# Idle matmuls where TensorE's array work runs low, and a new order of the steps, in a two-layer transformer kernel

## The reference

```python
x = x + 0.5 * ffn0(layernorm(x))            # gated, hidden 512, ternary weights times scales
x = x + attn0(layernorm(x))                 # linear attention, no softmax
x = x + 0.5 * ffn0(layernorm(x))            # the same weights again
x = x + 0.5 * experts(layernorm(x))         # 8 experts of rank 64, two picked by token 0 of a sequence
x = x + attn1(layernorm(x))                 # 16 heads of width 8, RoPE, causal softmax
x = x + 0.5 * experts(layernorm(x))
# ffn0: silu(x W1) * (x W2) -> gelu(. H1) -> gelu(. H2) -> . W3
```

## Time and profile before

| | |
|---|---|
| median of 3 runs | 642.38 us (640.28 to 642.96) |
| the profiled execution: its time | 645.81 us |
| its span, first to last instruction | 644.0 us |
| TensorE busy | 607.3 us (94%) |
| VectorE, ScalarE, GpSimd busy | 476.0, 479.9, 233.1 us |
| mean granted clock of TensorE | 0.984 |

### The profile page before, as it was taken

How to read it: one execution, slowest core, us unless ns; L and a number is a source line. 1 busy time by engine, 2 the same in 40 slices (tenths; PEclk the granted TensorE clock), 3 DMA queues, 4 the chain that set the end, 5 groups by cost and what they waited for, 6 DMA issues and landing times.

```text
span 644.0 us, 17311 instructions
## 1 busy us (share of the span) xinstructions
PE 607.3 (94%) x6902; PEld 472.0 (73%) x6902; DVE 476.0 (74%) x1298; ACT 479.9 (75%) x832; POOL 233.1 (36%) x354
## 2 busy tenths in 40 slices
PE   4899999999999999999999999998898999999997
PEld 3677878888887887888877887665565667766675
DVE  6667566765766778656777668898899787788964
ACT  5799778787788787887878776745778466778792
POOL 1402303312312526403337346756654542331032
PEclk9999999999999999999999999999999896899999
DMA  9300000000000001100003003413444423223002
GB/s 295 110 2 1 0 1 2 1 2 1 1 1 1 1 2 49 50 2 2 0 7 92 1 22 119 135 47 132 147 131 128 143 77 114 88 90 101 23 13 60
DMA packets 41230, 35.24 MB, mean 55 GB/s; under 512 B 2952, under 2 KB 37032, under 8 KB 41148
## 3 DMA queue, kind: packets, MB, share of 16 engines
q1 hardware_dynamic: 41148, 34.12, 16.8%
HBM read 19.17 MB, written 14.68 MB: 53 GB/s over the span
## 4 chain that ended last, share of the span: by engine, by line
PE 63%; DVE 14%; ACT 11%; issue 6%; POOL 2%; DMA 2%; SPq 1%; POOLq 0%; DVEq 0%; ACTq 0%
PE PSA L1009 20%; PE PSA L1013 19%; PE PSA L1248 5%; DVE MX L1438 3%; PE PSA L1028 3%; DVE G L1316 3%; ACT PB L1587 2%; ACT PSA L1492 2%; DVE RA L1431 2%; PE PSA L1236 2%; PE PSA L1227 1%; ACT G L1488 1%; PE PSA L1172 1%; PE PSA L1192 1%; PE PSA L1165 1%
## 5 line engine op out<-in xcount | busy, mean ns | idle before, releaser
L1009 PE MATMUL PSA<-ah,WH 128*128 128x512 f32 x320 | 130.5, 408 | 2.4 <-DVE al L1321 1.5
L1013 PE MATMUL PSA<-al,WH 128*128 128x512 f32 x320 | 125.1, 391 | 0.0
L1492 ACT ACTIVATE PSA<-PSA,SC 128x512 f32<-128x512 f32 x128 | 84.6, 661 | 50.8 <-PE PSA L1013 50.3
L1438 DVE TENSOR_REDUCE MX<-PSA 128x10 f32<-128x640 f32 x128 | 101.2, 815 | 17.7 <-PE PSA L1199 17.3
L1009 PE MATMUL PSA<-bh,WH 128*128 128x512 f32 x256 | 105.7, 413 | 3.1 <-DVE G L1316 3.1
L1013 PE MATMUL PSA<-bl,WH 128*128 128x512 f32 x256 | 100.2, 391 | 0.0
L1587 ACT ACTIVATE PB<-PSA 128x640 f32<-128x640 f32 x128 | 84.8, 703 | 20.3 <-PE PSA L1236 19.1
L1321 DVE TENSOR_TENSOR al<-PSA,ah 128x512 fp32r<-128x512 f32 x64 | 44.0, 688 | 56.5 <-ACT ah L1499 56.4
L1614 POOL TENSOR_SCALAR VE<-MV 128x4 f32<-128x4 f32 x46 | 11.2, 244 | 205.4 <-DVE MV L1291 205.4
L1009 PEld LDWEIGHTS PSA<-ah,WH 128*128 128x128 f32 x320 | 60.2, 188 | 17.6 <-DVE al L1321 3.8
L1013 PEld LDWEIGHTS PSA<-al,WH 128*128 128x128 f32 x320 | 60.2, 188 | 11.8 <-issue 1.0
(11 more groups left out here) (168 smaller groups left out, 1281.6 us busy)
## 6 DMA issues: line engine op xcount, KB each, us to landing
KQ<-dk SPq DMA_DIRECT2D x32, 192.0 KB
KQ<-dq SPq DMA_DIRECT2D x32, 192.0 KB
dk<-CB SPq DMA_DIRECT2D x16, 192.0 KB, 2.5
dq<-CB SPq DMA_DIRECT2D x16, 192.0 KB, 2.6
X<-in_x SPq DMA_DIRECT2D x8, 256.0 KB, 6.8
dk<-CB SPq DMA_DIRECT2D x16, 128.0 KB, 1.9
dq<-CB SPq DMA_DIRECT2D x16, 128.0 KB, 2.7
W<-in_w SPq DMA_DIRECT2D x3, 512.0 KB, 5.7
```

Source lines behind the costliest of these rows:

```text
L1009: e.matmul(o, WH[:, col:col + 128], hi, start=first, stop=False)
L1013: return e.matmul(o, WH[:, col:col + 128], low, start=False, stop=last)
L1438: e.tensor_reduce(MX[:, u % 2, :, :].rearrange("p t (l g) -> p l t g", l=2)[:, :, :, g], PSA[:, b:b + 2, 0:320].rearrange("p l (t k) -> p ...
L1492: e.activation(bank(b), bank(b), ACT.Gelu, scale=SC[:, k:k + 1]).then_inc(a_gelu, 1)
```

## The change

Four things. `fill` gets a larger share of a planned gap (FILLED 0.85, reserve SPARE 0.06 us plus the changes of tile shape) and a second form: between steps of 64-row tiles, when banks 6 and 7 are both unheld, four matmuls of 64x64 tiles and 256 columns take the place of the 128x128 one, so that the shape stays. A new function `hold` is called before each step of TensorE once the first stream of feed-forward work has ended: it adds up, by the new table WORK, what array work the plan has laid in the last HOLD[0] us and, where this is less than the share HOLD[1], it puts idle matmuls in front of the step, up to 0.5 us, and moves the planner's clock by them. The prices of some steps change (`expert`, `qk`, `value`, `vexp`, `max_out`, `pass2`, `weighed`, `upright`, `proj`, `lone_x`, `lone_g`). And SHIFT is a new set, so the order of all steps after the first ones is another. Three waits name their source's number instead of their own, which lets the half chunks of the ending pass each other.

```diff
@@ -69,23 +69,28 @@
     "att0": [("P", 1.08, 1.15), ("V", 0.6, 0.68)],
     "table": [("P", 1.1, 1.3), ("V", 0.6, 0.68)], "logit": [("P", 0.37, 0.55), ("V", 0.85, 0.95)],
     "tanh": [("A", 0.09, 0.2)], "gate": [("V", 0.14, 0.23)], "pick": [("G", 2.75, 2.82)], "pick_b": [("G", 1.25, 1.3)],
-    "expert": [("P", 0.42, 0.6), ("V", 0.33, 0.41)],
-    "qk": [("P", 0.95, 1.02), ("V", 1.9, 2.05)], "turned": [("G", 1.23, 1.27)],
+    "expert": [("P", 0.47, 0.66), ("V", 0.33, 0.41)],
+    "qk": [("P", 0.88, 1.06), ("V", 1.9, 2.05)], "turned": [("G", 1.23, 1.27)],
     "cast0": [("A", 0.52, 0.62), ("S", 0.95, 0.95), ("D", 2.5)], "rest0": [("G", 1.11, 1.16)],
     "cast1": [("A", 0.52, 0.62), ("S", 0.95, 0.95), ("D", 2.5)],
     "rest1": [("G", 1.12, 1.16), ("S", 0.95, 0.95), ("D", 2.3)], "reloc": [("S", 2.95, 2.95), ("D", 5.0)],
-    "value": [("P", 0.9, 1.1), ("A", 0.48, 0.59)], "vexp": [("A", 0.6, 0.7)], "rows": [("S", 0.65, 0.65), ("D", 2.0)], "ones": [("G", 1.15, 1.2)],
+    "value": [("P", 0.99, 1.16), ("A", 0.48, 0.59)], "vexp": [("A", 0.83, 0.9)], "rows": [("S", 0.65, 0.65), ("D", 2.0)], "ones": [("G", 1.15, 1.2)],
     "pass1": [("P", 0.225, 0.395), ("V", 0.735, 0.82)], "peak": [("V", 0.32, 0.4), ("A", 0.13, 0.24), ("G", 0.2, 0.26)],
-    "max_out": [("P", 0.22, 0.29), ("V", 0.33, 0.4), ("S", 1.18, 1.18), ("D", 3.8)],
-    "pass2": [("P", 0.22, 0.39), ("A", 0.58, 0.7)], "weighed": [("P", 1.12, 1.21), ("A", 0.27, 0.38)],
-    "upright": [("P", 0.45, 0.6), ("V", 0.65, 0.73)],
-    "flat": [("P", 0.27, 0.44), ("A", 0.27, 0.38)], "proj": [("P", 0.64, 0.71), ("V", 0.33, 0.41)], "store": [("S", 0.9, 0.9)],
+    "max_out": [("P", 0.12, 0.29), ("V", 0.33, 0.4), ("S", 1.18, 1.18), ("D", 3.8)],
+    "pass2": [("P", 0.22, 0.39), ("A", 0.6, 0.7)], "weighed": [("P", 1.13, 1.29), ("A", 0.27, 0.38)],
+    "upright": [("P", 0.49, 0.66), ("V", 0.65, 0.73)],
+    "flat": [("P", 0.27, 0.44), ("A", 0.27, 0.38)], "proj": [("P", 0.54, 0.71), ("V", 0.33, 0.41)], "store": [("S", 0.9, 0.9)],
     "half_stat": [("V", 0.85, 1.0)], "half_power": [("G", 0.8, 0.8)], "half_norm": [("V", 0.5, 0.6)],
     "half_xt": [("P", 0.3, 0.44), ("A", 0.27, 0.38)], "half_expert": [("P", 0.45, 0.71), ("V", 0.33, 0.42)],
     "half_store": [("S", 0.9, 0.9)],
-    "lone": [("P", 0.25, 0.4), ("A", 0.15, 0.2)], "lone_x": [("P", 0.4, 0.55), ("A", 0.15, 0.2)],
-    "lone_m": [("P", 0.2, 0.35), ("V", 0.1, 0.16)], "lone_g": [("P", 0.5, 0.6), ("V", 1.0, 1.1)],
+    "lone": [("P", 0.25, 0.4), ("A", 0.15, 0.2)], "lone_x": [("P", 0.6, 0.83), ("A", 0.15, 0.2)],
+    "lone_m": [("P", 0.2, 0.35), ("V", 0.1, 0.16)], "lone_g": [("P", 1.1, 1.37), ("V", 1.0, 1.1)],
     "lone_power": [("G", 0.7, 0.7)], "lone_df": [("V", 0.07, 0.15)],
+}
+WORK = {
+    "xtf": 0.43, "xta": 0.43, "xtp": 0.43, "up": 0.85, "hid": 0.85, "down": 0.85, "back": 0.43, "gram": 0.85, "half": 0.43,
+    "fold": 0.43, "att0": 0.85, "table": 0.43, "expert": 0.43, "qk": 0.85, "value": 0.85, "pass1": 0.15, "pass2": 0.16,
+    "weighed": 1.07, "upright": 0.43, "flat": 0.21, "proj": 0.43, "half_xt": 0.21, "half_expert": 0.43,
 }
 HOPS = {"P": 0.06, "V": 0.04, "A": 0.04, "G": 0.08, "S": 0.05}
 
@@ -104,27 +109,34 @@
 FIRST = (3, 1.5)
 LEAD = 20
 LONE = 4.0
-FILLED = 0.65
+HOLD = (3.4, 0.42)
+FILLED = 0.85
+SPARE = 0.06
 
...
-    ("after", 0, 2): -0.16, ("after", 0, 6): -0.02, ("after", 1, 7): 0.49, ("attend", 0): -0.02,
-    ("attend", 2): 0.1, ("attend", 3): 0.2, ("attend", 4): -0.16, ("attend", 5): -0.09, ("attend", 6): -0.19,
...
+    ("after", 0, 2): 0.16, ("after", 0, 3): 0.19, ("after", 0, 4): -0.1, ("after", 0, 6): -0.09,
+    ("after", 1, 0): -0.05, ("after", 1, 1): -0.29, ("after", 1, 4): -0.24, ("after", 1, 6): -0.38,
+    ("after", 1, 7): 0.09, ("attend", 0): -0.37, ("attend", 1): -0.15, ("attend", 2): 0.54, ("attend", 5): 0.08,
...
+    ("weigher", 9): 0.23, ("weigher", 10): 0.19, ("weigher", 12): 0.39, ("weigher", 13): -0.65,
+    ("weigher", 14): -0.14, ("weigher", 15): 0.23,
...
@@ -193,7 +205,8 @@
         self.added, self.picked = set(), {}
         self.into = [0, 0]
         self.lasts = 1
-        self.table = self.pe = ""
+        self.table = self.pe = self.last = ""
+        self.worked = []
         self.idle_from = 0.0
         self.lay()
 
@@ -235,28 +248,63 @@
                 t = max(t, later - 0.45 * (name == "up"))
             s0 = max((ready if name in BESIDE else t) + HOPS[eng], self.clock[eng])
             if eng == "P":
-                self.fill(s0)
-                self.idle_from = s0 + us
+                self.fill(s0, kind)
+                s0 = self.hold(s0, kind)
+                self.worked.append((s0, s0 + us, WORK.get(name, 0.0)))
+                self.idle_from, self.last = s0 + us, kind
             self.note(eng, s0, s0 + us, name)
             self.clock[eng] = s0 + us
             t = st.at[eng] = s0 + way[0]
         st.done = max([t] + [st.at[e] for e in st.at if name in BESIDE])
         return st
 
-    def fill(self, t):
-
-        free = {b: f for b, f in enumerate(self.bank) if f}
+    def keep(self, form, n, a, each, banks):
+        if n <= 0:
+            return
+        self.note("P", a, a + each * n, "keep" + form)
+        self.worked.append((a, a + each * n, n * {"h": 0.107, "f": 0.053, "w": 0.107}[form]))
+        k = self.count.get("keep", 0)
+        self.count["keep"] = k + 1
+        self.steps.insert(-1, Step("keep", k, x=n, b=min(banks), b2=max(banks), kind=form,
+                                   emptied=sum((self.bank[b] for b in banks), [])))
+
+    def fill(self, t, kind):
+
+        free = sorted((self.left(f), b) for b, f in enumerate(self.bank) if f)
         if not free or not self.opened:
             return
 
-        each = 0.06 if self.count.get("masks") else 0.23
-        b = min(free, key=lambda b: self.left(free[b]))
-        n = int((t - max(self.idle_from, self.left(free[b]) + 0.06) - 0.15) * FILLED / each)
-        if n > 1:
-            self.note("P", max(self.idle_from, self.left(free[b]) + 0.06), max(self.idle_from, self.left(free[b]) + 0.06) + each * n, "keep")
-            k = self.count.get("keep", 0)
-            self.count["keep"] = k + 1
-            self.steps.insert(-1, Step("keep", k, x=n, b=b, kind="w" if each > 0.1 else "", emptied=free[b]))
+        h = self.last == "h" and self.bank[6] is not None and self.bank[7] is not None
+        h = h and self.left(self.bank[6] + self.bank[7]) <= max(self.idle_from, free[0][0] + 0.1)
+        if h:
+            free = [(self.left(self.bank[6] + self.bank[7]), 6), (0.0, 7)]
+        form = "h" if h else "f" if self.count.get("masks") else "w"
+        each = {"h": 0.125, "f": 0.06, "w": 0.23}[form]
+        own = form if h else "f"
+        a = max(self.idle_from + 0.094 * (self.last != own), free[0][0] + 0.06)
+        n = int((t - a - 0.094 * (kind != own) - SPARE) * FILLED / each)
+        if n > (not h):
+            self.keep(form, n, a, each, [b for _, b in free[:1 + h]])
+
+    def hold(self, t, kind):
+
+        if len(self.dead) < 1 or kind not in "fh":
+            return t
+        done = 0.0
+        for a, z, work in reversed(self.worked):
+            if a < t - HOLD[0] - 4.0:
+                break
+            done += work * max(0.0, min(z, t) - max(a, t - HOLD[0])) / (z - a)
+        free = [b for _, b in sorted((self.left(f), b) for b, f in enumerate(self.bank) if f and self.left(f) + 0.06 < t)]
+        if kind == "h":
+            free = [b for b in free if b > 5]
+        short = HOLD[0] * HOLD[1] - done
+        if short <= 0.05 or len(free) <= (kind == "h"):
+            return t
+        each, work = (0.125, 0.107) if kind == "h" else (0.06, 0.053)
+        n = min(int(short / work + 0.99), int(0.5 / each))
+        self.keep(kind, n, t, each, free[:2 if kind == "h" else 1])
+        return t + each * n
 
     def note(self, eng, a, z, name):
         pass
@@ -1109,7 +1157,7 @@
                                      start=True, stop=True)
                     t.then_inc(p_logit, 1)
                 elif st.name == "half_xt":
-                    w.wait_ge(v_half_xn, n + 1)
+                    w.wait_ge(v_half_xn, st.src.n + 1)
                     emptied(w, st.emptied)
                     for j in range(2):
                         t = e.transpose(PSA[:, b, 128 * j:128 * j + 128], XN[:, st.i, j, :], IDN[:, :])
@@ -1206,8 +1254,14 @@
                         w.wait_ge(g_c, 5)
                     emptied(w, st.emptied)
                     for _ in range(st.x):
-                        ID = IDN if early else IDB
-                        e.matmul(PSA[:, b, 0:128], ID[:, :], ID[:, :], start=True, stop=True)
+                        if st.kind == "h":
+                            for x in range(2):
+                                for h in range(2):
+                                    e.matmul(PSA[64 * x:64 * x + 64, (st.b, st.b2)[h], 0:256], IM[64 * h:64 * h + 64, 0, 0:64],
```

(31 more changed lines are left out.)

## The result

The changed kernel is slower: 649.68 us median of 8 runs (647.91 to 650.17) against 642.51 us of the kernel before (638.05 to 646.95, 8 runs); ratio 1.0111, 95% interval 1.0082 to 1.014. I had forecast 638.5 us in 633.0 to 644.0.

A forecast was written before the change was run, and what follows sets the result against it. Bound: TensorE in the feed-forward chunks, shared in the attention, TensorE alone for 20.6 us at half clock. 645.8 - 6.1 + 1.0 + 0.5 - 1.0 = 640.2 us; middle with 636.8 taken: 638.5 us, range 633.0 to 644.0.

The forecast's parts named there:

- Part 3: New step prices and a new order of all steps, mainly in the attention; forecast to gain 1.0 us.
- Value: 1.0 us gained: Forecast for the new order, between 9 us better (VectorE's idle time after 551.3 us) and 2.9 us worse.
- bound for the worse: Near 430 us, where SP's queue is on the chain: one reloc more or less costs 2.9 us.
- Part 1: Idle matmuls from `hold` in the attention: 6.1 us saved by keeping the clock up, 1.0 us cost.
- 0.30 us for each us at the low level: Saving expected per us at 1.2 GHz, from VectorE's work in the two low stretches between 510.3 and 551.3 us.
- 6.1 us: Saving taken for 20.6 us at low clock between 510.3 and 551.3 us; bounds 2.1 and 8.7 us.
- the middle between 640.2 and 636.8: 638.5 us: whole kernel, if all or none of the profiled execution's 3.4 us above the median was low clock.
- Part 2: `fill` lays about 100 more idle matmuls in the attention, 5.7 us of array time; cost 0.5 us, bounds 0 and 5.7.
- 0.5 + 1.0: Forecast costs in us of the added idle matmuls: 0.5 for those of `fill`, 1.0 for those of `hold`.
- My sum for a gap of 1 us: In a planned TensorE gap, `fill` lays 0.80 x 0.85 instead of 0.85 x 0.65 us, 1.2 times as much.
- The idle matmuls stand on the path: Rival, chance 0.15: between 404 and 537.6 us some 160 more at 57 ns delay score groups; 646.1 us if all count.
- The new order gives more: Rival, chance 0.15: better prices bring VectorE to 0.88 after 551.3 us, worth 6 us; 633.5 us.

## Why the prediction was wrong

**The step that failed is Part 3, "Value: 1.0 us gained".** The new order costs 8.4 us at full clock; three pairs of kernels, with the old rule for idle matmuls, with the new one and with none, put the loss on the order. Its bound for the worse, one reloc, 2.9 us, was too near as well. I had argued that better prices give a better plan. But an order is found by a search, and the old list was the end of a good one: with the new prices the old offsets give a list that the planner ends at 640.8 us and the chip, at full clock, 7.5 us above the changed kernel. The new search climbed back only to 628.6 us against 623.1 us. With idle matmuls left out, the two lists are the same in their first 551 of 1735 steps, up to some 219 us of the plan, and differ from there.

How much of the 8.4 us the planner could have told is less sure. Its two ends are 5.5 us apart, but in different prices. If both lists are timed in one set of prices, step for step, without the pauses in which the planner finds no job, the new one ends 3.2 us later in the new prices (623.7 and 626.9) and 5.9 us in the old ones (621.1 and 627.0). So the planner holds 3 to 6 us. Some 2 to 2.6 us more are the maxima's transfer, which I had read in the chain of before ("two relocs stand ahead of the first `max_out`") and then priced by the number of relocs; that number is the same in both orders, and what had changed was the work left beside them. Only this second part is measured by an edit of its own. The first is the planner's figure, borne out by the ranking of five lists; in which places of the order it is lost stays open.

**Part 1, the price was right and the amount wrong.** 0.30 us for each us at the low level, from VectorE's work in rows of one execution, is 0.335 over 80. The estimate by the page "TensorE: Matmul & The Clock Gate" of the Trainium skill, section "HAM oscillation — how this bites in real kernels", half of the low stretch, is not what these runs show. But that execution had 21 us at the low level and the medians are 8 to 14. I saw that it stood above the runs, kept 6.1 us and then took the middle between 640.2 and 636.8, although by my own reasoning an excess that is clock leaves the sum at 640.2. With the medians the most that could be won was 642.5 - 638.2 = 4.3 us; the changed kernel, with 9.1 us left, won some 1 to 2 of them. And `hold` laid 8 matmuls, not 50: it counts `fill`'s idle matmuls as work. With that count left out, the planner of the changed kernel has it lay 58.

**Part 2 was right in kind.** 90 more by the new fill rule cost 0.8 us where I had 0.5; 0.5 + 1.0 for both kinds together against 2.5 us when 142 are laid. The cover is large but not free, 9 to 18 ns of each 57. My sum for a gap of 1 us was wrong: with no change of shape it gets 0.94 x 0.85 = 0.80 us in place of 0.55, 1.45 times as much and not 1.2. Still fewer were laid than I thought, 42 more up to 510.3 us and 122 in all, none in the 64-row form.

**The rivals.** "The idle matmuls stand on the path" gave the time nearest to the one that came, 646.1 us, by a mechanism that the runs refute. "The new order gives more" had the wrong sign. A rival "the new order is worse" was missing: I had let the search of before speak only against a gain. What transposes count for the clock no run here shows. One more thing I had not looked for: the changed kernel has 42 table loads on ScalarE where the one before has 36, the six more in the feed-forward stage, 7.7 us of ScalarE at 1283 ns each. That stage ends about 1 us later. Without idle matmuls its last matmul stands at 432.3 us in both orders, but there the profile of the old order had 3.4 us more at the low level before it. Whether the loads make that microsecond was not tested.

## What to carry to other kernels

Where a list of steps comes from a search, a change of its prices or rules is a new draw: work out what the planner itself ends at, before and after and in the same prices, and take a worse plan of several us as a forecast of a worse kernel. Lay idle matmuls into a finished order without letting them move the planner's clock; here they then cost a sixth to a third of their array time and gave about as much back. Read the clock of several runs, not of one profile, before pricing what it could give. And look at what work an order leaves beside its longest transfers; moving one transfer of the new order by hand gave it 3.7 us, all the idle matmuls that the change added gave 1.8, which is not clear of the noise.

## What was not expected of the hardware

The granted clock of one and the same kernel differs from run to run, 0 to 28 us at 1.2 GHz in 80 executions of one core, on each of four chips (0 to 22, 0 to 18, 1 to 28 and 0 to 22 us), and explains most of the spread of 637 to 647 us. A transfer of 2 x 8 KB took 7.06 us after its first issue to land behind eight transfers of 192 KB and two of a `spread`; with four of the eight put behind it, `pass2` could start 2.2 us sooner after the first issue.
